# Attention on one Trainium2 core: row maxima of a pair of heads spread over a longer stretch, value copies moved

## What is computed

```
q, k, v = x @ Wq, x @ Wk, x @ Wv            # per head: 2048 x 64
q, k    = rmsnorm(q, q_rms_w), rmsnorm(k, k_rms_w)
gate    = softplus(k . u_n / sqrt(64))       # one number per key and head
bias    = -max(i - j, 0) * omega_eff * gate[j]   # -inf where j > i
attn    = softmax(q @ k.T / sqrt(64) + bias)
y       = attn @ v ; x = layernorm(x + y @ Wproj)
```

## Time and profile before

| | us |
|---|---|
| median of 3 runs (3264.66 to 3268.54) | 3267.87 |
| the profiled execution: its own time | 3262.58 |
| the profiled execution: span from first to last instruction | 3260.8 |
| attention: first scores to last scores | 81.8 to 2114 |
| one pair of heads in the even part of attention | about 126 |

### The profile page before, as it was taken

How to read it: one execution, slowest core, us unless ns; L and a number is a source line. 1 busy time by engine, 2 the same in 40 slices (tenths; PEclk the granted TensorE clock), 3 DMA queues, 4 the chain that set the end, 5 groups by cost and what they waited for, 6 DMA issues and landing times. The chain is left out here.

```text
span 3260.8 us, 46767 instructions
## 1 busy us (share of the span) xinstructions
PE 3085.9 (95%) x15184; PEld 2404.4 (74%) x15184; DVE 1837.6 (56%) x4186; ACT 1839.4 (56%) x3185; POOL 1561.4 (48%) x1359
## 2 busy tenths in 40 slices
PE   4899999999999999999999999989999999999998
PEld 3767767767767677677676776678888888788887
DVE  7676677676666766776766767553333332332323
ACT  1677777777776777777777767743333332322222
POOL 5576676676665766766766666613212220000000
PEclk7999999999999999999999999989999999999999
DMA  2342332432432424324324326244434443121210
GB/s 79 71 107 50 86 79 55 105 70 66 103 83 71 98 50 94 74 59 105 70 66 105 69 65 158 70 123 137 121 91 120 116 116 116 57 78 39 71 47 20
DMA packets 210355, 273.95 MB, mean 84 GB/s; under 512 B 68992, under 2 KB 96768, under 8 KB 209984
## 3 DMA queue, kind: packets, MB, share of 16 engines
q1 hardware_dynamic: 210112, 270.97, 32.1%
HBM read 97.25 MB, written 55.90 MB: 47 GB/s over the span
## 5 line engine op out<-in xcount | busy, mean ns | idle before, releaser
L501 POOL TENSOR_TENSOR e_lo<-e_all,e_hi 128x512 fp32r<-128x512 f32 (+1 forms) x832 | 1032.6, 1249 | 612.5 <-ACT e_all L792 526.6
L792 ACT ACTIVATE e_all<-ps_s,bias 128x512 f32<-128x512 f32 (+3 forms) x1280 | 785.3, 624 | 170.7 <-PE ps_s L1134 92.4
L785 ACT ACTIVATE e_hi<-ps_s,bias 128x512 fp32r<-128x512 f32 (+1 forms) x832 | 561.3, 675 | 203.3 <-PE ps_s L1132 125.5
L998 DVE TENSOR_REDUCE maxes<-ps_m 128x1 f32<-128x512 f32 x768 | 516.2, 685 | 225.0 <-PE ps_m L1112 222.7
L1112 PE MATMUL ps_m<-k_ext,q_max 128*128 128x512 f32 (+3 forms) x1280 | 456.2, 379 | 57.7 <-DVE maxes L995 19.5
L1131 PE MATMUL ps_s<-q_twice,k_split 128*128 128x512 f32 (+3 forms) x1280 | 484.3, 378 | 21.3 <-ACT e_all L792 19.8
L1132 PE MATMUL ps_s<-q_ext,k_ext 128*128 128x512 f32 (+3 forms) x1280 | 469.0, 366 | 0.0
L1173 PE MATMUL ps_v<-e_lo,v_both 128*65 128x512 f32 (+1 forms) x832 | 431.4, 519 | 21.0 <-POOL e_lo L501 21.0
L1112 PEld LDWEIGHTS ps_m<-k_ext,q_max 128*128 128x128 f32 x1280 | 243.0, 190 | 219.8 <-DVE maxes L995 58.9
L995 DVE CUSTOM_DVE_ANT_0 ps_m<-ps_m,mask_row 128x128 f32<-128x128 f32 (+3 forms) x512 | 252.7, 495 | 231.0 <-PE ps_m L1112 229.3
L1152 PE MATMUL ps_v<-e_all,v_full 128*65 128x512 f32 (+2 forms) x896 | 324.0, 443 | 0.0
(11 more groups left out here) (234 smaller groups left out, 6566.9 us busy)
## 6 DMA issues: line engine op xcount, KB each, us to landing
q_twice<-q_max SPq DMA_DIRECT2D x256, 128.0 KB, 2.3
yt<-y_out SPq DMA_DIRECT2D x128, 130.0 KB
k_ext<-kq_hi SPq DMA_DIRECT2D x128, 128.0 KB, 2.3
q_max<-kq_hi SPq DMA_DIRECT2D x128, 128.0 KB, 2.4
k_split<-kq_hi SPq DMA_DIRECT2D x128, 128.0 KB, 2.4
k_split<-kq_lo SPq DMA_DIRECT2D x128, 128.0 KB, 2.4
q_ext<-kq_lo SPq DMA_DIRECT2D x128, 128.0 KB, 2.4
hidden<-gelu SPq DMA_DIRECT2D x64, 256.0 KB, 2.1
```

Of the source, the lines that this page charges most:

```text
L501: on.tensor_tensor(e_lo[:, i % LO_RING, off:QB], e_all[:, u_ % E_RING, off:QB], e_hi[:, i % HI_RING, off:QB].bitcast(F32), ALU.subtract).t ...
L785: nc.scalar.activation(e_hi[:, i % HI_RING, off:QB], ps_s[u_ % 2][:, off:QB], ACT.Exp, bias=by).then_inc(hi_done, 1)
L792: nc.scalar.activation(e_all[:, u_ % E_RING, off:QB], ps_s[u_ % 2][:, off:QB], ACT.Exp, bias=by).then_inc(ex_done, 1)
L998: nc.vector.tensor_reduce(maxes[:, qt, kc:kc + 1], ps_m[m % 2][:, 0:width], AX.X, ALU.max).then_inc(mx_free, 1)
```

## The change

The maxima of the first head of a pair are due from t0 - 0.495 to t0 + 0.44 in place of t0 + 0.24, those of the second from t0 + 0.48 to t0 + 1.44 in place of t0 + 0.27 to t0 + 1.08; the rule for n = 1 goes. GpSimd's five copies of values are due from t0 - 0.75 in steps of 0.14 for the first head (before: from t0 - 0.70 in steps of 0.04), and from t0 + 0.10 in steps of 0.036 for the second (before: from t0 + 0.05 in steps of 0.04). Number and kind of the instructions stay.

```diff
@@ attention_steps @@
             for i in range(5):
-                at((t0 - 0.70 if s == 0 else t0 + 0.05) + 0.04 * i, "values in", n, i)
+                at(t0 - 0.75 + 0.14 * i if s == 0 else t0 + 0.10 + 0.036 * i, "values in", n, i)
...
-            start, end = (turns[0] + 0.13, t0 + 0.24) if s == 0 else (t0 + 0.27, t0 + 1.08)
+            start, end = (turns[0] + 0.13, t0 + 0.44) if s == 0 else (t0 + 0.48, t0 + 1.44)
             for v, (qt, kc) in enumerate(MAXES):
                 qb = qt // TQ
                 when = max(start + (end - start) * v / (NM - 1), turns[qb] + 0.13)
...
-                if n == 1:
-                    when = max(0.48 + 0.60 * v / (NM - 1), turns[qb] + 0.13)
                 at(when, "max", n, v)
```

## The result

| | before | after |
|---|---|---|
| median of 4 runs each, us | 3268.20 | 3344.23 (3341.03 to 3347.55) |
| ratio, 95% interval | | 1.0233 [1.0215, 1.0251] |
| profiled execution: own time, span, us | 3262.58, 3260.8 | 3347.55, 3345.8 |
| first to last scores of attention, us | 2032 | 2116 |

The kernel is 2.3% slower. The loss lies in attention: 2116 - 2032 = 84 us of the 85 us by which the span grew.

What follows compares the result with a forecast made beforehand. PE is busy 95%, but in the gate stretch DVE's queue sets its pace, then SP's. Per pair 5.2 - 2.4 - 0.8 + 1.0 = 3.0 us, 45 over 15 pairs, less 2 in the last head: 3311 us, range 3212 to 3362.

Steps and rivals of the forecast that it cites:

- gate end: DVE, from the root to the gate's last transpose: 10 maxima in place of 4, ending 3.3 us later.
- first turn: PE's first turn of the next pair: behind the gate, a DVE reduction and 9.75 passes, 6.0 us later than before.
- scores of the last 512 queries: Second head's last scores on PE: 7.8 us later, since their row DMAs go behind two turns and weight loads.
- the wait inside it: PE's wait for the late row DMAs at the second head's last 512 queries: 2.2 us a pair.
- stretch, net of moved work: Root to the second head's last scores: 7.8 less 2.6 us of moved PE passes, 5.2 lost a pair, bounds 0.2 to 6.2.
- waits for maxima elsewhere: PE's waits for DVE's reductions outside the gate stretch: 2.4 us saved a pair, bounds 0 and 6.8.
- start of the first head: PE's wait for POOL's remainder, 1.5 us each: 0.8 us saved a pair through fewer maxima ahead of DVE's copy.
- SP in the second head: First head's third row group between second head's turns on SP delays copies: 1.0 us lost a pair, bounds 0 and 2.5.
- value copies: POOL's five copies of values per head only move, hidden in POOL's idle time: zero cost.
- The stretch has the room: Faster rival: turn under 0.5 us behind the gate's end, no wait at the later scores; 3221 us, chance 0.27.
- No change: Rival: gains and losses cancel within 6.5 us, if about 5 us a pair is saved outside the stretch; chance 0.08.
- The clock falls: Slower rival: waits drop PE to half clock, losing up to 3.4 us a stretch; 3362 us, chance 0.13.

Runs made afterwards that it cites:

- The added reductions alone: Kernel before plus six unused DVE reductions of 512 elements, one in each of the gate's parts 0 to 5: 3326.41 us, 1.0175.
- the gap: Kernel before with the second head's first 36 maxima at old density ahead of the gate, the last four behind it: 3303.76 us, 1.0111.
- the second head alone: Kernel before with only the second head's maxima moved as in the change, t0 + 0.48 to t0 + 1.44: 3332.80 us, 1.0210.
- the fastest run: Kernel before, second head's maxima ending at t0 + 0.98, DVE's gate-weight copy 0.04 heads earlier, POOL's weight split 0.02 later: 3233.97 us, 0.9898.
- both runs that tried it here: Last row DMAs queued ahead of both turns: kernel before with last four maxima behind the gate, 3308.54 us; changed kernel, maxima ending t0 + 1.37, 3373.44 us.
- a gate 2.8 us shorter: Kernel before with the second head's maxima ending at t0 + 0.98 in place of t0 + 1.08, none in the gate: 3257.05 us, 0.9966.

## Why the prediction was right

Forecast 3311 us, 3212 to 3362, slower with 0.65; measured 3344. The direction and both mechanisms held, the size was about half. Point by point, for one pair, in the pair at full clock (root at 564.4 us) against the pair of before shown above (root at 677.00 us). Where the table gives a stretch, it is the difference between the starts of its scores, less the PE passes that moved (0.23 us per 512 columns).

| step of the prediction | forecast | measured |
|---|---|---|
| gate end | +3.3 us | +2.9 |
| first turn | +6.0 | 587.84 - 564.4 - 17.29 = +6.1 |
| scores of the last 512 queries | +7.8 | 602.31 - 564.4 - 29.66 = +8.2 |
| the wait inside it | 2.2 | 2.25 |
| stretch, net of moved work | +5.2 | 8.2 - 2.6 = +5.6 |
| waits for maxima elsewhere and start of the first head | -2.4 - 0.8 | what the other rows leave: -2.1 |
| SP in the second head | +1.0 | +1.4 |
| value copies | 0 | 0 |
| sum | +3.0 | +4.9 |

The row for the scores, and for the wait, is this one, in the timeline of PE:

```profile
602.31 0.47 PE L1129 MATMUL ps_s<-q_twice,k_split 128*128 128x512 f32 x1 [2.25 <-DMA q_ext<-shift_rows]
```

**What held.** The stretch went as worked out: the gate that DVE's queue sets, the turn behind it, and the rows behind two turns. The added reductions alone and the gap show that each half costs time by itself (59 and 37 us; together, in the second head alone, 66). One sum of the prediction is off by 0.1: 12.4 - 0.53 - 0.51 + 0.46 gives 11.8, not 11.9; it changes nothing, since the rows come later than that.

**What was mis-sized.** Of the 42 us between the forecast of +43 and the +85 of the profiled execution, 1.9 x 15 = 28 us are terms; the clock below gave 21, and two pairs named there fell short. The gain outside the stretch came out 1.1 us a pair smaller, and both of its terms were too large. I counted on 0.8 us from "Start of the first head", where fewer maxima would let POOL's split begin sooner, and that wait is still 18.6 us in 14 places, 0.2 us less each. It belongs to the order of POOL's split and DVE's copy, as the fastest run shows. I counted on 2.4 us from "Waits for maxima elsewhere": the array's own waits outside the stretch were only 25.6 us before, 1.7 a pair, and fell to 10.1, a gain of 1.0; the 2.0 of the prediction was a mean over the whole span. The 0.9 us of the row beyond these two do not show in PE's idle brackets, and what they are stays open. The term of SP fits PE's waits for ACT's exponentials outside the stretch, which rose from 2.0 to 23.1 us, 1.4 a pair. The other 0.8 us are 0.4 in the stretch and 0.4 at SP.

**The clock.** I gave it 0.13 as a rival and 0 in the sum. It is part of the result: PE's busy time rose by 21.0 us over the same instructions. In the second pair above, the wait of 1.08 us at 709.69 and that of 2.49 us before 734.58 are followed by the first two of these stretches; the third follows the 2.25 us wait in the pair at full clock:

```profile
710.00:714.00 4.00, 4.00 (x13) 2.37 (x12) 3.79 (x12) 1.52 (x3) 1.27 (x2) 0.57 0.00 0
...
734.60:737.20 2.60, 2.60 (x6) 1.81 (x7) 0.00 (x0) 1.27 (x2) 0.00 (x0) 0.50 0.92 203
...
602.30:604.90 2.60, 2.59 (x13) 1.94 (x14) 0.92 (x3) 1.53 (x3) 0.46 (x1) 1.00 0.91 203
```

In the second PE's granted clock is 0.50, that is 1.2 GHz, and it does 6 instructions in 2.6 us; in the third it does 13 in 2.6 us at 1.00, 2.4 GHz. The first is mostly at the lower level. The Trainium skill (TensorE: Matmul & The Clock Gate, on HAM oscillation) says that waits for DMAs make the array's clock swing between its levels; the stretch behind the wait for the row DMAs agrees, the third shows that such a wait of about the same size does not always do it. My price for a whole pair, 3.4 us in every one, was too high: 21.0 / 15 = 1.4 us.

The terms and the clock make 4.9 x 15 + 21 = 94 us; the span grew by 85. Two pairs make up the difference: by the starts of their scores the first of the program grew by 1.1 us only, and the fifteenth, the one without a wait for the rows, became 0.3 us shorter. Why, was not taken apart.

**Rivals.** "The stretch has the room" falls at the point it named: the turn is 3.9 us behind the gate, not 0.5. "No change" needed 5 us a pair saved outside; it was 2.1. "The clock falls" came true beside the forecast, not in its place.

**The landing of the rows.** SP's timeline has the start of the last of the four row DMAs:

```profile
732.76 0.57 SPq L575 DMA_DIRECT2D q_ext<-shift_rows  x1
```

PE goes on at 734.58, 1.8 us later, where I took 1.5 from the earlier trace rows. The Trainium skill (DMA: Bandwidth & Descriptors, in the anatomy of one DMA) gives about 2.0 us as fixed cost, for DMAs from GpSimd; this measurement, from SP, lies nearer to it than to my row.

## What to carry to other kernels

A stretch that has little of one kind of work in it can be full on the engine that would have to take more: read the busy time and the idle brackets of that engine there before spreading work evenly into it. When several transfers on one queue are late together, changing their order may only change who waits, as in both runs that tried it here; look for a place where they are not due together. Look also for an in-order engine that stands idle for a small operation of another, with work queued behind it: moving two steps by 0.02 and 0.04 heads gave 23 us here, more than any other step tried.

## What the runs showed that was not expected

The cost of DVE work in the gate is not symmetric. Six operations of 0.6 us to the next start make the gate 3.6 us longer, and the kernel 59 us slower, 3.9 us a pair: at a granted clock of 1.00 a pair is 3.9 us longer than the one of before, and where the clock is a little lower, 5.8. Two pairs of that run:

```profile
489.88:619.94 130.06, 121.54 (x595) 90.37 (x594) 92.20 (x220) 93.13 (x165) 85.87 (x75) 1.00 0.33 76
749.66:881.66 132.00, 122.93 (x595) 91.21 (x594) 92.26 (x220) 93.04 (x165) 85.88 (x75) 0.99 0.32 75
```

The opposite, a gate 2.8 us shorter, leaves a regular pair as it was.

At the same place of neighbouring pairs of the changed kernel PE waits 1.08 us for DVE, at 578.24 and at 709.69. The stretch behind the second is at a clock of 0.57, as shown above; the one around the first is at 1.00:

```profile
577.00:581.00 4.00, 2.92 (x14) 1.90 (x14) 3.79 (x12) 1.52 (x4) 2.86 (x3) 1.00 0.00 0
```

So the length of the wait alone does not say whether the clock falls. What does, no run here shows.
